# Output projection in four parts, other places for the context transposes, other banks for the last values

## The chip, the core and the metric

The kernel runs on one core of one Trainium2 chip. Its five engines have queues of their own and work in order: PE (TensorE; PEld is its weight load), DVE (VectorE), ACT (ScalarE), POOL (GpSimd) and SP (SyncE, which here only issues DMAs). They meet through semaphores. PE writes to PSUM only, and the kernel uses PSUM as five tensors: psAB, psCD and psEF of two banks each, psO and psX of one bank each. The metric is the device time in microseconds; lower is better.

## The reference, cut to what matters

Eight batches of 256 tokens with 128 features attend to a context of 512 rows with 16 heads of 64, then go through a mixture of eight experts with a capacity of 160 slots each.

```
xn  = layernorm(layernorm(x)) ; q = xn @ w_q ; k, v = split(ctx @ w_kv)      # 16 heads x 64
attn = softmax(q * 64**-0.5 @ k.T) ; out = (attn @ v) @ w_out + b_out
x   = x + tanh(g_xattn) * tanh(gate) * out
t   = layernorm(x) ; expert = argmax(softmax(t @ gate_w)) ; pos = running count inside the expert
y   = relu(t @ w1[expert]) @ w2[expert] * prob      (dropped where pos >= 160)
x   = x + tanh(g_ffn) * y
```

## The kernel before, in words

**Slots.** The two heads that share 128 columns of the weights are a pair, so a batch has 8 pairs, and the kernel has 64 slots, numbered j; hp = j % 8 is the slot's place in its batch. "Slot 1 of batch 4" is hp 1 of the batch with index 4. All engines run the same loop `batch(b)` over slots, written out by hand; the order of the calls in it is the order on the engine.

**One slot on PE.** (1) Scores of pair j for two query tiles, in psAB and psCD. (2) Small work that depends on hp, in psO: ranks in slot 0, output projection in 1 and 3, x transposes in 4, token transposes in 5, logits in 6. (3) K and Q of pair j+2 in psEF (`k_project`, `q_project`). (4) `o_transposes`: the attention output of pair j-3 is transposed into the last 256 columns of psEF. (5) `v_project`: a fourth of half the values, in psX. (6) `values`: 48 matmuls of attention times values for pair j-2, in psO. In slot 2 of a batch the transposes of the next batch's context follow in psX (`ctx_transposes`).

**One slot on DVE.** Row maximum of psAB (L913, L916), low part of the values (VL, L906) out of psX, a small drain of psO that depends on hp, row maximum of psCD, `kq_lo` (HL, L900, or a copy to KQS, L896) out of psEF, in slot 1 `add_part` and in slot 3 `add_attention` out of psO, then `normalise_heads` (L924, L930) out of psO.

**One slot on ACT.** Two exponentials out of psAB (L753), `kq_hi` (L715) out of psEF, `phi` (L763), two exponentials out of psCD, `ot_copy` (L742), `v_hi` (L720), `phi`. `kq_hi` waits for `o_transposes` of the same slot, since both use psEF. POOL makes the low half of the probabilities (L654), and SP transposes both halves by DMA (PT<-PARTS, L477), two DMAs a slot; `values` two slots later reads what they bring.

**Who may use psO.** `wait_o(free_when)` waits until the last tenant of psO has been read, and notes what will free it from the new one; `wait_x` does the same for psX. So the next tenant of psO on PE always waits for the engine that drains the last one.

**The projection.** out @ w_out sums over all 8 pairs. Before, `project_part` (L1353) takes pairs 0 to 3 of batch b-1 in slot 1 of batch b, and DVE's `add_part` (L957) adds the result to X1; `project` (L1389) takes pairs 4 to 7 in slot 3, and `add_attention` (L946) makes the new x. In the last batch the parts stand behind the slots, in psX and psEF.

Of the kernel before, what the change touches and what calls it, by code (L numbers as in the profile page):

```python
# [21 lines left out]
F32 = mybir.dt.float32  # L22
# [11 lines left out]
def gated_block(nc, x, ctx_1024, g_xattn, g_ffn, ln_gamma, ln_beta, w_q, w_kv, w_out, b_out, gate,  # L34
# [34 lines left out]
    with ExitStack() as ctx:  # L69
# [122 lines left out]

        def ps_logits(b):
            return (psX if b == B - 1 else psO)[:, 0:QT * E]

        def ps_ranks(b):
            return (psX if b == B - 1 else psO)[:, 0:(QT + 1) * E]
# [166 lines left out]
        PART_STEP, CTX_STEP, PROJECT_STEP = 1, 2, 3  # L364
        VALUES_BEHIND = 2

# [22 lines left out]

        def kq_bank(j):  # L390

            return psCD if j == 1 else psEF
# [14 lines left out]
        BO_STEP, BIAS_STEP = 2, 7  # L407
# [280 lines left out]
        def _(act):  # L688
# [15 lines left out]
            def ctxt_hi(b):  # L704
                act.wait_ge(ctxt_psum, b + 1)
                act.activation(cT_hi[:, b % 2, :], psX[:], ACT.Copy).then_inc(ctxt_hi_done, 1)
# [27 lines left out]
            def ot_copy(n, bank=psOT, pairs=1):  # L734
# [4 lines left out]
                if b:  # L739

                    act.wait_ge(part_psum if pair < PAIRS // 2 else proj_psum, b)
# [41 lines left out]
            def batch(b):  # L783
                for j, hp in slots(b):
                    if hp == CTX_STEP + 1 and not is_last(b):
# [4 lines left out]
                    if hp == CTX_STEP:  # L790
                        v_hi(*v_group(b, hp))
# [5 lines left out]
                    if hp != CTX_STEP and v_group(b, hp):  # L797
# [39 lines left out]
        def _(dve):  # L837
# [47 lines left out]
            def ctxt_lo(b):  # L885
                dve.wait_ge(ctxt_hi_done, b + 1)
                dve.tensor_tensor(cT_lo[:, b % 2, :], psX[:], cT_hi[:, b % 2, :].bitcast(F32), ALU.subtract).then_inc(ctxt_lo_done, 1)
# [30 lines left out]
            def normalise_heads(b, hp):  # L918

                j = b * PAIRS + hp  # L920
                sums = psO[:, 0:2 * QT * (DH + 1)].rearrange("p (g d) -> p g d", d=DH + 1)
                n = turn(j)
                dve.wait_ge(pv_done, n)
                dve.reciprocal(rden[:, hp % 2, :], sums[:, :, DH]).then_inc(rden_done, 1)  # L924
# [9 lines left out]
            def add_attention(b, banks=None):  # L934

                dve.wait_ge(proj_psum, b + 1)
                dve.wait_ge(part_done, B + 1 if is_last(b) else b + 1)
# [13 lines left out]
            def add_part(b, part, bank=psO):  # L951

                dve.wait_ge(part_psum, part + 1)
# [113 lines left out]
            def batch(b):  # L1067
                for j, hp in slots(b):
                    row_max(b, hp, 0)
                    if hp == CTX_STEP + 1:  # L1070
                        if not is_last(b):
                            ctxt_lo(b + 1)
                    elif j and v_group(*back(b, hp, 1)):
                        v_lo(*v_group(*back(b, hp, 1)))
                    if hp == RANKS_STEP and b > 1:
# [17 lines left out]
                    if j == LAST:  # L1093
                        low_parts()
                        place(B - 2)
# [493 lines left out]
```

## Time and profile before

| | |
|---|---|
| median of 3 runs | 491.48 us (490.69 to 491.77) |
| the profiled execution: its time, its span | 489.88 us, 487.9 us |
| busy: PE, DVE, ACT, POOL | 433.6, 367.0, 382.9, 355.7 us |
| granted TensorE clock, mean | 0.994 |

Busy time is the union of an engine's instructions, and a matmul's duration holds the filling of the pipeline, so matmuls overlap in the rows: what one costs PE is read from the starts that follow each other. In the timeline a row has start, duration, engine, line, operation, tiles and count; in brackets the idle time of the engine just before it and what ended it. "SPq" rows are the time in which SP issues a DMA, not the transfer. In the table of stretches each row begins with the stretch and its length, and the busy time of each engine follows.

### The profile page before, as it was taken

How to read it: one execution, taken by the hardware profiler on the slowest of the kernel's cores; microseconds unless marked ns; L12 is line 12 of the kernel's file. 1: busy time of each engine (PE TensorE's matmuls, PEld its weight loads, DVE VectorE, ACT ScalarE, POOL GpSimd, SP SyncE). 2: the span in 40 equal slices, each digit the busy share in tenths (PEclk: the TensorE clock that was granted, in tenths of full speed). 3: DMA queues.
4: the chain of work that ended last, by engine and by line, in shares of the span. 5: the costliest groups of instructions: out<-in, count | busy, mean ns of one | idle time of the engine just before them, and what ended most of it. 6: DMA issues, size and time to landing. Idle time of an engine off the chain costs nothing.

```text
span 487.9 us, 13156 instructions
## 1 busy us (share of the span) xinstructions
PE 433.6 (89%) x5096; PEld 334.3 (69%) x5096; DVE 367.0 (75%) x803; ACT 382.9 (78%) x616; POOL 355.7 (73%) x270
## 2 busy tenths in 40 slices
PE   8869998899889998899889989899889989888893
PEld 7647775676667776676667767677667666657893
DVE  4788886699678886789669887689669867785622
ACT  5879997699778988699788987799779986893330
POOL 3785894788867987798867987788778876681325
PEclk9998999999999999999999999999999999999999
DMA  6399999899998999999989999999989997797021
GB/s 181 128 206 174 184 205 156 162 199 196 194 184 179 193 192 170 187 186 202 190 180 176 179 186 184 195 188 196 190 129 177 192 179 138 124 165 163 14 65 44
DMA packets 283037, 82.10 MB, mean 168 GB/s; under 512 B 264387, under 2 KB 280435, under 8 KB 282976
## 3 DMA queue, kind: packets, MB, share of 16 engines
q1 hardware_dynamic: 281600, 77.96, 89.7%
q0 software_dynamic: 1376, 3.30, 2.1%
q8 instruction: 41, 0.67, 0.6%
q14 instruction: 20, 0.16, 0.1%
HBM read 10.83 MB, written 5.14 MB: 33 GB/s over the span
## 4 chain that ended last, share of the span: by engine, by line
PE 53%; DVE 18%; ACT 12%; DMA 7%; issue 6%; POOL 3%; POOLq 0%; SPq 0%; ACTq 0%; DVEq 0%
DVE MXL L913 7%; DMA PT<-PARTS 6%; PE psO L1299 5%; ACT P L753 4%; PE psAB L1267 4%; PE psO L1301 4%; ACT HL L715 4%; PE psO L1300 4%; PE psAB L1274 4%; PE psCD L1274 3%; DVE HL L900 3%; PE psEF L1193 3%; PE psO L1389 3%; PE psO L1353 3%; PE psEF L1195 2%
## 5 line engine op out<-in xcount | busy, mean ns | idle before, releaser
L654 POOL TENSOR_TENSOR PARTS<-P,PARTS 128x1024 f16<-128x1024 f32 x125 | 267.2, 2140 | 78.3 <-ACT PARTS L763 77.6
L763 ACT ACTIVATE PARTS<-P 128x1024 f16<-128x1024 f32 x126 | 135.3, 1074 | 0.8
L1299 PE MATMUL psO<-VH,PT 128*128 128x65 f16 x1008 | 99.6, 195 | 26.6 <-DVE row L946 11.5
L1299 PEld LDWEIGHTS psO<-VH,PT 128*128 128x128 f16 x1008 | 90.9, 98 | 46.6 <-DVE row L946 14.6
L753 ACT ACTIVATE P<-psAB,NB 128x512 f32<-128x512 f32 x128 | 81.5, 694 | 42.4 <-DVE NB L916 41.1
L1300 PE MATMUL psO<-VL,PT 128*128 128x64 f16 x1008 | 99.0, 193 | 0.0
L1301 PE MATMUL psO<-VH,PT 128*128 128x65 f16 x1008 | 98.8, 194 | 0.0
L913 DVE TENSOR_REDUCE MXL<-psAB 128x2 f32<-128x1024 f32 x64 | 78.3, 1223 | 19.5 <-PE psAB L1274 12.3
L1301 PEld LDWEIGHTS psO<-VH,PT 128*128 128x128 f16 x1008 | 92.0, 97 | 0.0
L1300 PEld LDWEIGHTS psO<-VL,PT 128*128 128x128 f16 x1008 | 91.9, 99 | 0.0
L753 ACT ACTIVATE P<-psCD,NB 128x512 f32<-128x512 f32 x128 | 81.0, 692 | 1.5 <-DVE NB L916 0.7
L913 DVE TENSOR_REDUCE MXL<-psCD 128x2 f32<-128x1024 f32 x64 | 77.6, 1213 | 0.2 <-PE psCD L1274 0.2
L900 DVE TENSOR_TENSOR HL<-psEF,HL 128x768 fp32r<-128x768 f32 x41 | 39.2, 955 | 26.5 <-ACT HL L715 24.7
L715 ACT ACTIVATE HL<-psEF 128x768 fp32r<-128x768 f32 x41 | 33.4, 814 | 19.0 <-PE psEF L1310 18.6
L906 DVE TENSOR_TENSOR VL<-psX,VH 128x512 f16<-128x512 f32 x63 | 42.8, 680 | 1.5 <-ACT VH L720 1.5
L1274 PE MATMUL psAB<-HL 64*128 64x512 f32 x252 | 41.2, 432 | 0.8 <-ACT P L753 0.8
L1274 PE MATMUL psCD<-HL 64*128 64x512 f32 x252 | 37.5, 402 | 4.2 <-ACT P L753 4.2
L720 ACT ACTIVATE VH<-psX 128x512 f16<-128x512 f32 x63 | 38.8, 616 | 0.0
L924 DVE RECIPROCAL rden<-psO 128x4 f32<-128x4 f32 x64 | 11.4, 179 | 35.2 <-PE psO L1301 34.6
L1193 PE MATMUL psX<-w_hi,cT_hi 128*128 128x512 f32 x63 | 30.2, 479 | 5.0 <-DVE VL L906 2.6
L742 ACT ACTIVATE OT<-psEF 128x256 f32<-128x256 f32 (+1 forms) x63 | 25.1, 399 | 9.1 <-PE psEF L1310 7.2
L1274 PEld LDWEIGHTS psCD<-HL 64*128 64x128 f32 x252 | 22.5, 186 | 14.3 <-ACT P L753 10.2
(228 smaller groups left out, 876.5 us busy)
## 6 DMA issues: line engine op xcount, KB each, us to landing
ctx_raw<-in_ctx_dram SPq DMA_DIRECT2D x8, 256.0 KB, 3.6
w1s<-in_L_ffn_w_dram SPq DMA_DIRECT2D x8, 256.0 KB, 3.4
w2s<-in_L_ffn_w_dram SPq DMA_DIRECT2D x8, 256.0 KB, 4.4
PT<-PARTS SPq DMA_TRANSPOSE x126, 4.8
experts_table<-zeros POOLq DMA_DIRECT2D x2, 645.0 KB, 4.1
X<-in_x_dram SPq DMA_DIRECT2D x8, 128.0 KB, 4.0
wraw<-in_L_xattn_w_kv_dram SPq DMA_DIRECT2D x4, 256.0 KB, 5.1
out_dram<-row SPq DMA_DIRECT2D x8, 128.0 KB, 2.8
```

Source lines behind the costliest of these rows:

```text
L654: pool.tensor_tensor(PARTS[:, par, qt, 1], P32[:, par, qt], PARTS[:, par, qt, 0], ALU.subtract).then_inc(plo_done, 1)
L715: act.activation(HL[:, hp % 2, H_KHI:H_KHI + KQ], kq_bank(j)[:, 0:KQ], ACT.Copy).then_inc(kq_hi_done, 1)
L753: last = act.activation(P32[:, par, qt, SK * h:SK * h + SK], score_bank(qt)[:, SK * h:SK * h + SK], ACT.Exp, bias=NB[:, par, qt, h:h + 1])
L763: act.activation(PARTS[:, hp % 2, qt, 0], P32[:, hp % 2, qt], ACT.Copy).then_inc(phi_done[qt], 1)
L900: dve.tensor_tensor(hl[:, H_KLO:H_KLO + KQ], kq_bank(j)[:, 0:KQ], hl[:, H_KHI:H_KHI + KQ].bitcast(F32), ALU.subtract).then_inc(kq_done, 1)
L906: dve.tensor_tensor(VL[:, kt, 8 * half:8 * half + 8, :], bank[:].rearrange("p (h d) -> p h d", d=DH), VH[:, kt, 8 * half:8 * half + 8, 0:D ...
L913: dve.tensor_reduce(MXL[:, par, qt, :, 0], score_bank(qt)[:].rearrange("p (h n) -> p h n", h=2), AX.X, ALU.max, negate=True).then_inc(max_ ...
L1193: pe.matmul(dst, hi_l, hi_r, start=True, stop=False)
L1274: last = pe.matmul(score_bank(qt)[:, SK * h:SK * h + SK], hl[rows, q + P * qt:q + P * qt + P], hl[rows, k:k + SK], start=(q == H_QHI and k ...
L1299: pe.matmul(psO[:, g:g + DH + 1], phi, VH[:, kt, head, 0:DH + 1], start=first_, stop=False)
L1300: pe.matmul(psO[:, g:g + DH], phi, VL[:, kt, head, :], start=False, stop=False)
L1301: last = pe.matmul(psO[:, g:g + DH + 1], plo, VH[:, kt, head, 0:DH + 1], start=False, stop=last_)
```

## The change

1. The projection is made in four parts of two pairs each. Parts 0 and 1 (pairs 0, 1 and 2, 3) stand in slots 5 and 7 of the batch itself, part 2 (pairs 4, 5) in slot 1 of the next batch, and the rest (pairs 6, 7, with `add_attention`) in slot 3. PE does each behind K and Q and ahead of `o_transposes`; before, it did them ahead of K and Q.
2. DVE does `add_part` and `add_attention` right behind the second row maximum, ahead of `kq_lo`; before, behind it.
3. The context transposes of batches 1 to 7 go to psO, behind the scores of slot 2, ahead of K and Q. ACT's `ctxt_hi` moves from slot 3 to the head of slot 2, DVE's `ctxt_lo` from slot 3 to slot 2. With this `v_hi` and `v_lo` of slot 2 stand where they stand in every other slot.
4. In the last batch: logits and ranks of batch 6 use psEF; the part of eight matmuls behind the last scores is gone (slots 5 and 7 hold it now); `values` of the last pair goes to psX.
5. POOL adds the projection's bias to X1 in slot 4 instead of slot 7, and `ot_copy` waits for the part that reads its place.

```diff
-        PART_STEP, CTX_STEP, PROJECT_STEP = 1, 2, 3
+        CTX_STEP, PROJECT_STEP = 2, 3
+        PART_STEPS = {5: (0, 0), 7: (0, 1), 1: (1, 2)}
+        PARTS_A_BATCH = 3
+        def part_of(b, hp):
+            late, n = PART_STEPS.get(hp, (0, None))
+            return None if n is None or b < late else (b - late, n)
+        def part_pairs(n):
+            return range(2 * n, 2 * n + 2)
+        def ctx_bank(b):
+            return psO if b else psX
-        BO_STEP, BIAS_STEP = 2, 7
+        BO_STEP, BIAS_STEP = 2, 4
...
 # ACT, batch()
-                    if hp == CTX_STEP + 1 and not is_last(b):
+                    if hp == CTX_STEP and not is_last(b):
                         ctxt_hi(b + 1)
...
 # DVE, batch()
+                    if part_of(b, hp):
+                        add_part(*part_of(b, hp))
+                    if hp == PROJECT_STEP and not is_first(b):
+                        add_attention(b - 1)
                     if not (is_last(b) and hp + AHEAD >= PAIRS):
                         kq_lo(*next_pair(b, hp, AHEAD))
-                    if hp == PART_STEP and not is_first(b):
-                        add_part(b - 1, b - 1)
-                    if hp == PROJECT_STEP and not is_first(b):
-                        add_attention(b - 1)
...
 # PE
-            def project_part(b, pairs, bank=psO):
+            def project_part(b, n, bank=psO):
+                pairs = part_pairs(n)
                 if bank is psO:
-                    wait_o((part_done, b + 1))
+                    wait_o((part_done, PARTS_A_BATCH * b + n + 1))
                 pe.wait_ge(ot_done, b * PAIRS + pairs[-1] + 1)
                 pe.wait_ge(wo_in, 16)
...
 # PE, batch()
-                    if hp == PART_STEP and not is_first(b):
-                        project_part(b - 1, range(PAIRS // 2))
-                    if hp == PROJECT_STEP and not is_first(b):
-                        project(b - 1)
+                    if hp == CTX_STEP and not is_last(b):
+                        ctx_transposes(b + 1)
...
                         q_project(*next_pair(b, hp, AHEAD))
+                    if part_of(b, hp):
+                        project_part(*part_of(b, hp))
+                    if hp == PROJECT_STEP and not is_first(b):
+                        project(b - 1)
...
 # PE, behind the last slot
                     values(b, PAIRS - 3)
-                    project_part(b, range(PAIRS // 2), psX)
-                    values(b, PAIRS - 1)
+                    values(b, PAIRS - 1, psX)
```

PE in slot 1 of batch 4, before: the projection (psO<-wo,OT) stands between the scores (psCD<-HL) and K and Q (psEF).

```order
L1274 MATMUL psCD<-HL 128x512 x6
L1353 MATMUL psO<-wo,OT 128x128 x8
L1193 MATMUL psEF<-cT_hi,w_hi 128x512
L1194 MATMUL psEF<-cT_lo,w_hi 128x512
L1195 MATMUL psEF<-cT_hi,w_lo 128x512
L1193 MATMUL psEF<-xT_hi,w_hi 128x256
L1194 MATMUL psEF<-xT_lo,w_hi 128x256
L1195 MATMUL psEF<-xT_hi,w_lo 128x256
L1310 MATMUL psEF<-ident,O 128x128 x2
```

The same place now:

```order
L1292 MATMUL psCD<-HL 128x512 x6
L1211 MATMUL psEF<-cT_hi,w_hi 128x512
L1212 MATMUL psEF<-cT_lo,w_hi 128x512
L1213 MATMUL psEF<-cT_hi,w_lo 128x512
L1211 MATMUL psEF<-xT_hi,w_hi 128x256
L1212 MATMUL psEF<-xT_lo,w_hi 128x256
L1213 MATMUL psEF<-xT_hi,w_lo 128x256
L1373 MATMUL psO<-wo,OT 128x128 x4
L1328 MATMUL psEF<-ident,O 128x128 x2
```

The projection has moved behind the six matmuls of K and Q and has four matmuls instead of eight.

DVE in slot 1 of batch 4, before: from the row maximum of psCD to the normalisation (rden, O); HL is `kq_lo`, X<-psO is `add_part`.

```order
L913 TENSOR_REDUCE MXL<-psCD 128x2
L916 TENSOR_REDUCE NB<-MXL 128x2
L900 TENSOR_TENSOR HL<-psEF,HL 128x768
L957 SCALAR_TENSOR_TENSOR X<-psO,gscale,X 128x256
L924 RECIPROCAL rden<-psO 128x4
L930 TENSOR_TENSOR O<-psO,rden 128x2x2x64
```

The same place now:

```order
L931 TENSOR_REDUCE MXL<-psCD 128x2
L934 TENSOR_REDUCE NB<-MXL 128x2
L978 SCALAR_TENSOR_TENSOR X<-psO,gscale,X 128x256
L918 TENSOR_TENSOR HL<-psEF,HL 128x768
L944 RECIPROCAL rden<-psO 128x4
L950 TENSOR_TENSOR O<-psO,rden 128x2x2x64
```

`add_part` and `kq_lo` have changed places; slot 3 differs in the same way for `add_attention`, and slots 5 and 7 gain an `add_part` at this place.

ACT in slot 2 and the beginning of slot 3 of batch 4, before: cT_hi is `ctxt_hi`, VH is `v_hi`.

```order
L753 ACTIVATE P<-psAB,NB 128x512 x2
L715 ACTIVATE HL<-psEF 128x768
L720 ACTIVATE VH<-psX 128x8x64
L763 ACTIVATE PARTS<-P 128x1024
L753 ACTIVATE P<-psCD,NB 128x512 x2
L742 ACTIVATE OT<-psEF 128x256
L763 ACTIVATE PARTS<-P 128x1024
L706 ACTIVATE cT_hi<-psX 128x512
L753 ACTIVATE P<-psAB,NB 128x512 x2
```

The same slot now:

```order
L723 ACTIVATE cT_hi<-psO 128x512
L773 ACTIVATE P<-psAB,NB 128x512 x2
L732 ACTIVATE HL<-psEF 128x768
L783 ACTIVATE PARTS<-P 128x1024
L773 ACTIVATE P<-psCD,NB 128x512 x2
L762 ACTIVATE OT<-psEF 128x256
L737 ACTIVATE VH<-psX 128x8x64
L783 ACTIVATE PARTS<-P 128x1024
```

`ctxt_hi` has moved from the end of the slot to its head, ahead of the first exponentials, and `v_hi` from ahead of the second exponentials to behind them.

## Rows read from the trace of the kernel before

**Rows 1.** Stretches of batch 4: slots 1 and 3, and all eight slots.
```profile
232.38:241.35 8.97, 7.33 (x87) 5.79 (x85) 5.22 (x9) 7.22 (x11) 6.87 (x6) 1.00 1.16 187
...
248.06:257.43 9.37, 7.72 (x93) 6.14 (x89) 5.99 (x16) 6.88 (x11) 6.89 (x6) 1.00 0.73 153
...
sum 53.90, PE 49.42 PEld 37.33 DVE 43.06 ACT 46.08 POOL 43.43; mean PE 6.18 PEld 4.67 DVE 5.38 ACT 5.76 POOL 5.43
```

**Rows 2.** Timeline of PE in slot 1 of batch 4: start, duration, what.
```profile
232.96 2.05 PE L1353 MATMUL psO<-wo,OT 128*128 128x128 f32 x16
234.77 0.47 PE L1193 MATMUL psEF<-cT_hi,w_hi 128*128 128x512 f32 x1
...
236.59 0.40 PE L1195 MATMUL psX<-w_hi,cT_lo 128*128 128x512 f32 x1
...
238.63 0.20 PE L1299 MATMUL psO<-VH,PT 128*128 128x65 f16 x1 [1.65 <-DVE X L957]
...
240.17 0.70 PE L1267 MATMUL psAB<-wraw 64*128 64x512 f32 x2
```

**Rows 3.** Timeline of DVE and ACT in slot 1 of batch 4.
```profile
235.56 0.16 DVE L916 TENSOR_REDUCE NB<-MXL 128x2 f32<-128x4 f32 x1
237.22 0.96 DVE L900 TENSOR_TENSOR HL<-psEF,HL 128x768 fp32r<-128x768 f32 x1 [1.51 <-ACT HL L715]
238.10 0.47 DVE L957 SCALAR_TENSOR_TENSOR X<-psO,gscale,X 128x256 f32<-128x256 f32 x1
...
236.38 0.81 ACT L715 ACTIVATE HL<-psEF 128x768 fp32r<-128x768 f32 x1 [1.29 <-PE psEF L1310]
```

**Rows 4.** Waits: who waited, for whom, total us, times, longest.
```profile
PE psO L1299 <- DVE row L946: 11.5, 7, 1.7
PE psO L1299 <- DVE X L957: 11.5, 7, 1.7
...
PE psX L1219 <- DVE VL L906: 3.9, 6, 0.7
...
PEld psO L1299 <- DVE winners L994: 1.4, 1, 1.4
```

**Rows 5.** Timeline of PE in slot 3 of batch 7: second scores.
```profile
409.58 0.96 PE L1274 MATMUL psCD<-HL 64*128 64x512 f32 x6 [0.65 <-ACT P L753]
```

**Rows 6.** Timeline of DVE in slot 5 of batch 4.
```profile
264.79 0.41 DVE L883 COPY tT<-psO 128x256 f32<-128x256 f32 x1
...
266.36 0.16 DVE L916 TENSOR_REDUCE NB<-MXL 128x2 f32<-128x4 f32 x1
```

**Rows 7.** Timeline of SP's queue, slots 1 to 7 of batch 4 and beyond.
```profile
245.42 1.55 SPq L452 DMA_DIRECT2D X<-in_x_dram  x1
...
253.08 0.80 SPq L484 DMA_DIRECT2D ctx_raw<-in_ctx_dram  x1
...
260.77 1.85 SPq L459 DMA_DIRECT2D w2s<-in_L_ffn_w_dram  x2
...
268.88 1.00 SPq L448 DMA_DIRECT2D out_dram<-row  x1
...
281.57 0.73 SPq L459 DMA_DIRECT2D w2s<-in_L_ffn_w_dram  x1
282.40 17.42 SPq L477 DMA_TRANSPOSE PT<-PARTS  x6
```

**Rows 8.** Batch 0: SP's issue of w_out, its landing on the page, PE in slot 5.
```profile
47.54 0.61 SPq L489 DMA_DIRECT2D wo<-in_L_xattn_w_out_dram  x1
...
wo<-in_L_xattn_w_out_dram SPq DMA_DIRECT2D x1, 512.0 KB, 5.3
...
49.61 0.38 PE L1310 MATMUL psEF<-ident,O 128*128 128x128 f32 x2
```

**Rows 9.** Timeline behind the last slot: DVE's last low half, PE's last values.
```profile
442.90 1.21 DVE L1020 TENSOR_TENSOR wraw<-psCD,wraw 128x1024 f16<-128x1024 f32 x1
...
447.16 0.20 PE L1299 MATMUL psO<-VH,PT 128*128 128x65 f16 x1 [0.48 <-DVE O L930]
```

More of the change, by code:

```diff
@@ L948, in add_attention, with add_part @@
                                          op1=ALU.add).then_inc(x1_done, 1)
-            def add_part(b, part, bank=psO):
+            def add_part(b, n, bank=psO):
+                part = PARTS_A_BATCH * b + n
                 dve.wait_ge(part_psum, part + 1)
@@ L1069, in batch @@
                     row_max(b, hp, 0)
[L1070 to L1073, printed above, removed]
+                    if j and v_group(*back(b, hp, 1)):
                         v_lo(*v_group(*back(b, hp, 1)))
+                    if hp == CTX_STEP and not is_last(b):
+                        ctxt_lo(b + 1)
                     if hp == RANKS_STEP and b > 1:
@@ L1276, in scores, with values @@
                 last.then_inc(score_psum, 1)
-            def values(b, hp):
+            def values(b, hp, bank=psO):
                 j = b * PAIRS + hp
                 par = hp % 2
-                wait_o((norm_done, turn(j)))
+                (wait_x if bank is psX else wait_o)((norm_done, turn(j)))
                 if j == 0:
@@ L1298, in values @@
                             first_, last_ = kt == 0, kt == KT - 1
-                            pe.matmul(psO[:, g:g + DH + 1], phi, VH[:, kt, head, 0:DH + 1], start=first_, stop=False)
-                            pe.matmul(psO[:, g:g + DH], phi, VL[:, kt, head, :], start=False, stop=False)
-                            last = pe.matmul(psO[:, g:g + DH + 1], plo, VH[:, kt, head, 0:DH + 1], start=False,
+                            pe.matmul(bank[:, g:g + DH + 1], phi, VH[:, kt, head, 0:DH + 1], start=first_, stop=False)
+                            pe.matmul(bank[:, g:g + DH], phi, VL[:, kt, head, :], start=False, stop=False)
+                            last = pe.matmul(bank[:, g:g + DH + 1], plo, VH[:, kt, head, 0:DH + 1], start=False,
                                              stop=last_)
@@ L1387, in project @@
                     dst = psO[:, D * qt:D * qt + D]
-                    for pair in range(PAIRS // 2, PAIRS):
-                        last = pe.matmul(dst, OT[:, pair * QT + qt, :], wo[:, pair, :], start=(pair == PAIRS // 2),
+                    for pair in range(PAIRS - 2, PAIRS):
+                        last = pe.matmul(dst, OT[:, pair * QT + qt, :], wo[:, pair, :], start=(pair == PAIRS - 2),
                                          stop=(pair == PAIRS - 1))
```

59 lines of the change are left out of this document (33 added, 26 removed).

## The prediction

> **What bounds the kernel now.** I read the table of stretches first, slot by slot over one batch in the steady part. The reader is to see there that the slots are not alike: slot 1 takes 8.97 us and slot 3 9.37 us, the other six (53.90 - 8.97 - 9.37) / 6 = 5.93 us on the mean, and that PE, the busiest engine, is busy for 49.42 of the batch's 53.90 us [rows 1]. So PE sets the pace, with 4.48 us of gaps a batch, and the long slots are where the gaps should be looked for. The timeline of PE in slot 1 then shows where. The projection takes PE from 232.96 to the start of K at 234.77, 1.81 us for 16 instructions (8 matmuls, each in two passes); the last V matmul starts at 236.59, and the values start only at 238.63, after 1.65 us without work, released by DVE's `add_part`. The values then hold PE until 240.17, 1.54 us [rows 2]. Third, DVE and ACT at the same place tell why the add is late: DVE is done with the second row maximum at 235.56 + 0.16 = 235.72, but the instruction next in its queue is `kq_lo`, and that waits 1.51 us for ACT's `kq_hi`, which itself waited 1.29 us for the transposes behind K and Q. The add, 0.47 us long, stands behind it and starts at 238.10 [rows 3]. Its own operand, the projection, was ready before K began at 234.77. The list of waits shows that this is not one slot: 11.5 us over 7 slots behind `add_part`, 11.5 us over 7 behind `add_attention`, and 3.9 us over 6 for the context transposes, which wait until DVE has emptied psX [rows 4].
>
> **The change part by part, ordinary batches (1 to 6).** PE's work stays the same: 16 projection matmuls a batch before (8 and 8), 16 now (4 in each of four slots), so the 0.91 us (half of 1.81) that slots 1 and 3 each lose, slots 5 and 7 each gain. What changes is waits.
>
> *Slot 1.* With four matmuls fewer the last V matmul starts at 236.59 - 0.91 = 235.68 and is through some 0.23 later (the step from one 512-column matmul to the next), at 235.9. DVE is free for the add at 235.72, its operand is there (the part now stands ahead of the transposes and V, which are nearly through by then), and it ends at 235.72 + 0.47, with the handing over about 236.25. So the values begin at about 236.2 to 236.3 instead of 238.63, and of the 1.65 us wait about 0.3 is left; in a slot whose V is a little later less. I take 0.2 for each of the four slots with a part. What is late next is DVE's add itself, not `kq_lo`: that now ends behind the start of the values, beside 1.54 us of them. Queued behind the add on DVE are `kq_lo` (wanted by the scores two slots on) and the normalisation, which waits for the values anyway; both have that cover, and without it the 0.47 us would show once a slot.
>
> *Slot 3.* The same edit, the same wait: 1.65 us goes, 0.2 stays.
>
> *Slots 5 and 7.* Their 0.91 us of matmuls are already in the balance of PE's work. In slot 5 the part may only enter psO when DVE has copied the token transposes, at 264.79 + 0.41 = 265.20. Behind it PE has 0.91 us of part and about 0.9 of transposes and V (an estimate: K, Q, transposes and V take 236.59 + 0.23 - 234.77 = 2.05 together [rows 2]), so it wants the values' bank at about 267.0. DVE's second row maximum ends at 266.36 + 0.16 = 266.52 [rows 6], the add at about 267.05: the copy and the add cost PE no more than they do in slot 1. Slot 7 has no other tenant in psO. The bounds for the wait in each of the four slots are nothing and the present 1.65; near 0.2 is where the rows of slots 1 and 5 both put it.
>
> *Slot 2.* The context transposes wanted psX empty and waited 0.65 us (3.9 over 6) [rows 4]; in psO they stand behind the scores, and the normalisation before them is done meanwhile, so that wait goes. ACT pays: `ctxt_hi` must now wait until PE has done scores and transposes, ahead of the first exponentials, while `v_hi` no longer stands ahead of the second ones. If these come late, the second scores of slot 3 wait for them. In batch 7, where slot 2 has no context transposes and is short already, such a wait is seen, 0.65 us [rows 5]. Its bounds are nothing and that 0.65; I take 0.35, near the middle.
>
> *SP and DMA.* Nothing is added to SP's queue, but it must keep up. Bounds: nothing from below, 1.3 a batch from above (rival 1); I take 0.3, nearer to the low end, since the change makes the fast slots 5 and 7 slower and so evens out the demand.
>
> Sum of an ordinary batch: -1.65 - 1.65 - 0.65 + 4 x 0.2 + 0.35 + 0.3 = -2.5 us, over six batches -15.0.
>
> **Batch 0.** Here the change adds a wait that no other batch has. Part 0 now needs w_out in slot 5 of batch 0; SP issues that load at 47.54 and such a load lands 5.3 us later, about 52.85, while PE reaches the place of the part at 49.61 [rows 8]. That is 3.2 us of stall, with everything of PE queued behind it: the transposes for `kq_lo`, V, and the values of the slot. The parts of slots 5 and 7 add 0.91 us each, and slots 1 and 3 of this batch have none to lose. SP's queue is solid in that stretch and catches up meanwhile, so I give back 0.6: 3.2 + 1.8 - 0.6 = +4.4. The bounds are +1.5 (the stall wholly given back by later slots that wait for transposes now) and +5.0.
>
> **Batch 7 and the tail.** Slots 1 and 3: two waits less the 0.4 that stay, -2.9, and half of each projection gone, -1.8. Slot 5 +0.95. Slot 6: the logits leave psO, and the values no longer wait for DVE's reading of them (1.4 us on PE's weight load [rows 4], of which I take 0.8, since transposed probabilities land hardly earlier). Slot 7's part stands where PE waits for the last exponentials: nothing. Behind the slots, the eight-matmul part goes, and the values of the last pair enter psX instead of waiting for psO. They then wait for the last low half, at 442.90 + 1.21 = 444.11, for their second half alone, and end at about 444.11 + 0.1 + 0.77 = 445.0; with 0.38 for a pair of transposes (as in rows 8) the next values start at 445.4 instead of 447.16 [rows 9], -1.8. Sum -2.9 - 1.8 + 0.95 - 0.8 - 1.8 = -6.35.
>
> Moving the bias on POOL from slot 7 to slot 4 costs nothing: it stands there ahead of an idle wait for `phi`, and the first reader is slot 5; without that cover it would be one 128x256 addition a batch.
>
> Total: -15.0 + 4.4 - 6.35 = -16.95. Against the profiled execution's own time of 489.88 us (487.9 of span and 2.0 around it) that is 472.9; the median of the runs, 491.48, lies 1.6 above, so 474.5.
>
> **Rivals.**
> 1. *SP's queue becomes the bound.* From 282.40 to 299.82 SP issues six transposes one behind the other, 17.42 us, 2.90 each. Sixteen a batch take 46.5 us, and the other issues (1.55 + 0.80 + 1.85 + 1.00 + 0.73 = 5.9) make it 52.4 [rows 7]. PE's own need by my sum is 53.90 - 2.8 = 51.1 before any wait for DMA. If SP can't do better when pressed, a batch gains 1.5, not 2.5: -9.0, with batch 0 at +3.3 (the parts hide in it) and batch 7 at -5.4: -11.1, 480. Against it: the stretch is the fullest of the batch, and slots of even length press the queue less.
> The Trainium skill bears on this in "Perfetto Trace Analysis", section "What 'DMA-bound' means": a kernel is DMA-bound on the sequencer when the issuing engine's track is solid DMA slices. The trace has such a track in the stretch named, not in slots 1 to 4. The skill's "DMA: Bandwidth & Descriptors", section "Latency and other measured facts", gives 261 GB/s for a DMA transpose; the 512 KB of one would take 2.0 us by it, an estimate from that page, and a batch 38 us, which binds nothing and leaves 474.5. The 2.90 us measured here decide, so the rival stays.
> 2. *All gaps of PE close.* 53.90 - 49.42 = 4.48 a batch, -26.9 in six, batch 7 -8.0 (its 6.35 and the waits left in it), batch 0 +3.3: -31.6, 460. For it speaks that the gaps named are nearly all there are; against it, ACT (46.08 us busy a batch [rows 1]) and SP have little room for it.
> 3. *psO becomes a serial bank, and it is slower.* psO has four projections, the context and the small work now, each to be drained before the values. If in each slot w us of wait stay, a batch changes by -3.95 + 4w: from w = 1.0 on it gains nothing, and with w = 1.65, the present wait, it loses 2.65. Over seven batches +18.6, with the stall of batch 0 and the tail +20: 512. What would do it is DVE reaching the second row maximum late in these slots. Against it: in slots 1 and 5 DVE is done with it before PE's V would be through.
> The Trainium skill speaks for this rival ("Perfetto Trace Analysis", section "Matmuls"): independent matmul groups should rotate through different banks, so that the drain of one overlaps the next. By that rule the parts belong in another bank; the trace shows K, Q and V, which use psEF and psX, between part and values, and that is the cover the price w depends on.
> 4. *No change*: batch 0's stall and SP's queue eat the gain, 491.
>
> **How the numbers follow.** The forecast, 468 to 480, has 0.55; SP's queue (480, up to 486) 0.20; all gaps closed (460) 0.15; psO serial (512) 0.07; no change 0.03. Faster by over 0.2% (about what a measurement of this kernel can tell from no change): 0.55 + 0.20 + 0.15 = 0.90; same 0.03; slower 0.07. The range 463 to 485 leaves out the last two, half of the closed gaps and the edge of SP's case, just under 0.2.
>
> **What would show it.** In the profile after, slots 1 and 3 should be about 6.5 us long, slots 5 and 7 about 6.6; the waits of the values for `add_part` and `add_attention` should be under 0.5 us each; PE should stand still for about 3 us near 50 us, waiting for w_out; SP's queue should be fuller. I am wrong if the values wait over 1 us for the add in slots 5 or 7, if the values wait for transposes all along, or if slot 2 is longer than 6.7 us.

## The result and the profile after

The changed kernel takes 471.93 us (median of 4 runs, 470.05 to 474.06) where the kernel before, run beside it, takes 491.41. The ratio is 0.9607, 95% interval 0.9561 to 0.9652. The profiled execution took 471.12 us, of which 469.1 are span. A few runs of some kernels were slow (over 1.5% above the fastest of the same kernel, at a lower granted clock): the medians below are of all runs, the ratios leave the slow ones out, and the profile of experiment 3 is of one of them.

First the table of stretches of batch 4, slots 1, 3, 5, 6 and 7 and the sum of all eight, which answers to [rows 1].

```profile
229.20:235.73 6.53, 6.21 (x77) 4.69 (x75) 5.23 (x11) 6.34 (x12) 4.54 (x5) 1.00 0.98 191
...
241.49:248.77 7.28, 6.98 (x85) 5.46 (x85) 6.08 (x16) 6.66 (x13) 6.56 (x5) 1.00 1.13 187
...
254.19:261.06 6.87, 6.72 (x83) 5.59 (x85) 5.50 (x10) 6.84 (x13) 6.87 (x6) 1.00 1.02 226
261.06:268.55 7.49, 6.16 (x75) 4.52 (x73) 5.34 (x14) 5.31 (x9) 5.74 (x3) 1.00 1.19 184
268.55:275.31 6.76, 6.76 (x78) 4.61 (x75) 5.87 (x14) 5.36 (x11) 4.38 (x4) 1.00 1.36 201
sum 51.78, PE 49.54 PEld 37.16 DVE 44.00 ACT 44.94 POOL 42.79; mean PE 6.19 PEld 4.64 DVE 5.50 ACT 5.62 POOL 5.35
```

PE's work is unchanged (49.54 us against 49.42), and the batch is 2.1 us shorter. Slots 1 and 3 have lost 2.4 and 2.1 us, slots 5 and 7 are longer. Slot 6 is new among the long ones: 7.49 us, with PE busy for only 6.16.

PE in slot 1 of batch 4, which answers to [rows 2]: the part, the last V matmul, the first of the values.

```profile
230.72 1.05 PE L1373 MATMUL psO<-wo,OT 128*128 128x128 f32 x8
...
232.29 0.40 PE L1213 MATMUL psX<-w_hi,cT_lo 128*128 128x512 f32 x1
233.01 0.20 PE L1317 MATMUL psO<-VH,PT 128*128 128x65 f16 x1 [0.32 <-DVE X L978]
```

DVE at the same place, which answers to [rows 3].

```profile
232.36 0.16 DVE L934 TENSOR_REDUCE NB<-MXL 128x2 f32<-128x4 f32 x1
232.47 0.48 DVE L978 SCALAR_TENSOR_TENSOR X<-psO,gscale,X 128x256 f32<-128x256 f32 x1
232.93 0.96 DVE L918 TENSOR_TENSOR HL<-psEF,HL 128x768 fp32r<-128x768 f32 x1
```

The add now follows the second row maximum at once, and PE stands for 0.32 us where it stood for 1.65. `kq_lo` begins when the values do.

The list of waits (engine, tile and line, for whom: us in total, times, longest) answers to [rows 4]. A wait of the values is booked on PE or, where the weight load was held, on PEld.

```profile
PEld psCD L1292 <- ACT P L773: 15.2, 24, 2.0
...
PEld psO L1317 <- DVE X L978: 9.6, 21, 0.8
...
PE psO L1317 <- DMA PT<-PARTS: 5.2, 9, 1.1
PE psCD L1292 <- ACT P L773: 5.1, 15, 1.6
...
PE psO L1373 <- DMA wo<-in_L_xattn_w_out_dram: 4.3, 1, 4.3
...
PEld psO L1317 <- DVE row L966: 1.9, 7, 0.3
...
PE psO L1317 <- DVE X L978: 1.6, 5, 0.3
```

Before, the weight load's line beside the 11.5 us of PE was:

```profile
PEld psO L1299 <- DVE X L957: 14.6, 7, 2.1
```

The waits for the adds are short. One wait can stand in both lists: before, a wait of 1.65 us on PE was 2.08 on the weight load, so 0.4 us on the weight load costs PE nothing. Of the 21 waits for `add_part` on the weight load, five are waits of PE too, 0.33 us each, in slot 1 of batches 2 to 6. PE's timeline says the same: from V's last matmul to the first of the values it takes 0.24 us in a slot without an add, and in these batches 0.72 in slot 1, 0.36 in slot 7 and 0.24 in slots 3 and 5.

One wait is new, and one has grown. PE waits 4.3 us, once, for w_out. And the values wait for transposed probabilities 9 times, 5.2 us in all, up to 1.1; in the trace of before this line reads 1.7 us, 4 times. Slot 6 of batch 4 holds two of them, in PE's timeline:

```profile
264.90 0.19 PE L1317 MATMUL psO<-VH,PT 128*128 128x65 f16 x1 [0.58 <-DMA PT<-PARTS]
...
266.54 0.20 PE L1317 MATMUL psO<-VH,PT 128*128 128x65 f16 x1 [0.76 <-DMA PT<-PARTS]
```

The wait for w_out has a second price. These two stretches, from 47.2 and from 52.1 us, show it (behind the length stand the busy times of PE, PEld, DVE, ACT and POOL, then the granted clock):

```profile
47.20:51.50 4.30, 0.02 (x1) 0.00 (x0) 1.14 (x2) 3.13 (x5) 4.30 (x3) 1.00 0.98 196
52.10:55.40 3.30, 3.30 (x25) 2.68 (x24) 1.44 (x2) 0.69 (x2) 0.00 (x0) 0.50 1.19 145
```

PE stands still in the first, and in the second the granted clock is 0.50, the 1.2 of the two levels 1.2 and 2.4 GHz: V's matmuls start 0.43 us apart there, against 0.23 in slot 1 of batch 4.

SP's queue in and behind batch 4, which answers to [rows 7], has few gaps:

```profile
224.04 18.91 SPq L494 DMA_TRANSPOSE PT<-PARTS  x6
...
256.52 1.14 SPq L476 DMA_DIRECT2D w2s<-in_L_ffn_w_dram  x2
257.76 6.86 SPq L494 DMA_TRANSPOSE PT<-PARTS  x2
...
276.86 17.41 SPq L494 DMA_TRANSPOSE PT<-PARTS  x6
```

A row of six holds the gaps between its issues too: the six from 224.04 are 15.9 us of issue in 18.9, those from 276.86 are 16.0 in 17.4, so 2.6 to 2.7 each. I add up SP's issues from batch to batch, without gaps: in batches 2 to 5 they fill 92 to 95% of the time, in the kernel before 79 to 85%. The mean issue of a transpose grows from 2.45 to 2.73 us in these batches. And the queue is behind what feeds it: over batches 1 to 6, POOL's low half is done 0.73 us before SP begins its transpose (the median; 0.02 in the kernel before), so it is not POOL that is late.

Measured from one row maximum of psAB to the next, the slots have lengths that repeat to 0.1 us where nothing disturbs them. Means over batches 1 to 6, and the usual length of after:

| slot | 0 | 1 | 2 | 3 | 4 | 5 | 6 | 7 | batch |
|---|---|---|---|---|---|---|---|---|---|
| before | 5.69 | 8.96 | 6.71 | 9.37 | 5.43 | 5.84 | 6.01 | 5.80 | 53.80 |
| after | 5.63 | 6.53 | 5.78 | 7.35 | 5.62 | 6.87 | 6.26 | 7.08 | 51.12 |
| after, undisturbed | 5.67 | 6.53 | 5.77 | 7.25 | 5.43 | 6.87 | 5.82 | 6.76 | 50.10 |

So the span's 18.8 us come from batches 1 to 6 (-16.1), batch 7 and what follows (-7.4), batch 0 (+4.3) and the start (+0.4).

### The profile page after: what moved, and what is told of

Read it like the earlier page. It is cut to its first block, busy times and chain, and to the rows that moved or that the text cites. A ratio compares the mean times of both kernels' runs of the same rounds, so it can differ in the third digit from the quotient of the medians.

```text
span 469.1 us, 13202 instructions
## 1 busy us (share of the span) xinstructions
PE 434.6 (93%) x5096; PEld 334.6 (71%) x5096; DVE 372.3 (79%) x818; ACT 383.3 (82%) x616; POOL 355.1 (76%) x270
## 4 chain that ended last, share of the span: by engine, by line
PE 36%; DVE 18%; POOL 17%; DMA 10%; issue 9%; ACT 9%; SPq 1%; POOLq 0%; ACTq 0%; DVEq 0%
POOL PARTS L671 14%; DMA PT<-PARTS 8%; DVE MXL L931 7%; ACT P L773 4%; PE psO L1317 3%; PE psAB L1285 3%; PE psO L1373 3%; PE psO L1319 2%; PE psO L1318 2%; DVE HL L918 2%; PE psCD L1285 2%; PE psCD L1292 2%; PE psEF L1211 2%; PE psEF L1549 2%; DVE VL L924 2%
## 5 line engine op out<-in xcount | busy, mean ns | idle before, releaser
L773 ACT ACTIVATE P<-psAB,NB 128x512 f32<-128x512 f32 x128 | 81.7, 698 | 25.1 <-DVE NB L934 24.9
L1292 PE MATMUL psCD<-HL 64*128 64x512 f32 x252 | 38.5, 410 | 5.3 <-ACT P L773 5.1
L944 DVE RECIPROCAL rden<-psO 128x4 f32<-128x4 f32 x63 | 11.4, 180 | 27.5 <-PE psO L1319 27.1
```

The lines of the kernel that those rows point to most:

```text
L773: last = act.activation(P32[:, par, qt, SK * h:SK * h + SK], score_bank(qt)[:, SK * h:SK * h + SK], ACT.Exp, bias=NB[:, par, qt, h:h + 1])
L1292: last = pe.matmul(score_bank(qt)[:, SK * h:SK * h + SK], hl[rows, q + P * qt:q + P * qt + P], hl[rows, k:k + SK], start=(q == H_QHI and k ...
```

## The experiments

All times are medians; the ratios are to the kernel before on the same chip, with their 95% intervals. "After" is 0.9607. What is read from a profile is read from one execution of each kernel.

**1. The order on DVE alone, in the kernel before.**

```diff
 # DVE, batch()
+                    if hp == PART_STEP and not is_first(b):
+                        add_part(b - 1, b - 1)
+                    if hp == PROJECT_STEP and not is_first(b):
+                        add_attention(b - 1)
                     if not (is_last(b) and hp + AHEAD >= PAIRS):
                         kq_lo(*next_pair(b, hp, AHEAD))
                     if hp == CTX_STEP:
                         v_lo(*v_group(b, hp))
-                    if hp == PART_STEP and not is_first(b):
-                        add_part(b - 1, b - 1)
-                    if hp == PROJECT_STEP and not is_first(b):
-                        add_attention(b - 1)
```

> The kernel before with one edit: DVE does add_part and add_attention ahead of kq_lo; the projection stays in two parts of eight matmuls, ahead of K and Q, in slots 1 and 3. Theory (the late add in DVE's queue is the cause of the long slots): both 1.65 us waits of the values vanish, in seven batches 23 us at the most; some of it comes back as waits for transposed probabilities, since SP's queue has less slack: 468 to 476 us, with no wait for w_out in batch 0. Rival (the split into four, or the place behind K and Q, is what helps): the values then wait for something else in slots 1 and 3, and the time stays above 484 us.

473.56 us, 0.9636 (0.9598 to 0.9673). In the list of waits the two lines of 11.5 us are gone, and this line has come up:

```profile
PE psO L1299 <- DMA PT<-PARTS: 8.5, 12, 1.7
```

Four moved lines give nearly all that the whole change gives; the intervals of the two overlap. Undisturbed, slots 1 and 3 are 7.16 and 7.56 us long, 1.8 less each than before, and the sum of the eight is 50.1, as in the kernel after. With eight matmuls on PE the add is done before V is through: the values follow V's last matmul by 0.24 us in slots 1 and 3, as in a slot without an add, so no wait is left.

**2. The old order on DVE, in the kernel after.**

```diff
-                    if part_of(b, hp):
-                        add_part(*part_of(b, hp))
...
-                    if hp == PROJECT_STEP and not is_first(b):
-                        add_attention(b - 1)
                     if not (is_last(b) and hp + AHEAD >= PAIRS):
                         kq_lo(*next_pair(b, hp, AHEAD))
+                    if part_of(b, hp):
+                        add_part(*part_of(b, hp))
+                    if hp == PROJECT_STEP and not is_first(b):
+                        add_attention(b - 1)
```

> The kernel after with one edit: the adds are put back behind kq_lo on DVE, all four of a batch. Theory (the place in DVE's queue is the price of a tenant of psO): each of the 28 adds makes the values wait about 1.4 us longer, 39 us in all, some of it beside waits that are there anyway: 500 to 512 us, slower than the kernel before. Rival (the parts of four matmuls are early enough for the old order too): under 10 us on 472.

507.23 us, 1.0350 (1.0327 to 1.0372), slower than the kernel before. PE's first values and DVE's add in slot 1 of batch 4:

```profile
251.61 0.20 PE L1317 MATMUL psO<-VH,PT 128*128 128x65 f16 x1 [1.65 <-DVE X L978]
```

```profile
250.20 0.96 DVE L918 TENSOR_TENSOR HL<-psEF,HL 128x768 fp32r<-128x768 f32 x1 [0.41 <-ACT HL L732]
251.08 0.47 DVE L978 SCALAR_TENSOR_TENSOR X<-psO,gscale,X 128x256 f32<-128x256 f32 x1
```

The same 1.65 us as in the kernel before, with half the matmuls, and in slots 1, 3 and 7 instead of two (0.8 in slot 5): batches of 55.9 us. The wait belongs to the place in DVE's queue, and the split alone makes it worse.

**3. w_out loaded at the start.**

```diff
             sp.dma_start(ctx_raw[:], ctx_t[1]).then_inc(ctx_in, 16)
+            sp.dma_start(wo[:], w_out.rearrange("(c p) n -> p c n", p=P)).then_inc(wo_in, 16)
...
-                    if is_first(b) and hp == WO_STEP:
-                        sp.dma_start(wo[:], w_out.rearrange("(c p) n -> p c n", p=P)).then_inc(wo_in, 16)
```

> The kernel after with one edit: SP issues the load of w_out at the start, behind the second context, and not in slot 5 of batch 0. Theory (the stall of PE for w_out in batch 0 is lost time): it goes, 4.3 us in the trace, so 3.3 to 4.3 us faster than the kernel after, about 468 us. Rival (PE's stall lets SP's queue catch up, and SP sets the pace behind it): the waits for transposes take its place, and the gain is under 1.5 us.

465.29 us, 0.9499 (0.9462 to 0.9535). Slot 5 of batch 0 falls from 12.52 to 6.38 us, and the time by about 5 (0.0108 of 490). The stall was lost time, and SP's catching up did not pay for it. It cost 6.1 us of slot 5 where PE stood for 4.3; in this profile the granted clock stays 1.00 there, and the other 1.8 us are about what 3.4 us at half the clock lose, so I put them down to the clock of 0.50 behind the stall.

**4. The context transposes at their old place, in psX at the end of slot 2** (with `ctxt_hi`, `ctxt_lo`, `v_hi` and `v_lo` as before).

```diff
-            return psO if b else psX
+            return psX
...
-                    if hp == CTX_STEP and not is_last(b):
-                        ctx_transposes(b + 1)
                     if hp == X_STEP and not is_last(b):
...
                         values(*back(b, hp, VALUES_BEHIND))
+                    if hp == CTX_STEP and not is_last(b):
+                        ctx_transposes(b + 1)
```

> The kernel after with one edit: the context transposes go back to the end of slot 2 in psX, with ctxt_hi and ctxt_lo in slot 3 and v_hi, v_lo of slot 2 at their old places. Theory (the wait for psX was lost time): 0.65 us in each of six or seven batches comes back, and the ACT wait in slot 3 (0.3) goes: +2 to +4 us, 474 to 476. Rival (SP's queue now sets the pace, and what PE gains in slot 2 is lost in waits for transposes): within 1 us of the kernel after.

474.21 us, 0.9664 (0.9630 to 0.9697): 2.8 us above after by the ratios, but the intervals overlap, so the time does not show it. The wait for psX is back:

```profile
PE psX L1242 <- DVE VL L926: 4.4, 7, 0.7
```

Slot 2 grows from 5.77 to 6.72 us and slot 3 shrinks from 7.25 to 6.94, 0.6 us a batch in all. The 0.3 us in slot 3 is the price that ACT pays. That is without disturbance. As they ran, batches 1 to 6 are 51.26 us on the mean, against 51.12 in after, and the values wait 2.2 us for transposes here, 5.2 in after: most of what the place in psO saves was lost there again, as the rival said. And 4.7 of the 5.7 us by which this profile's span is longer lie in batch 0, where the granted clock fell to 0.50 twice more than in after.

**5. The last values in psO again.**

```diff
-            normalise_heads(B - 1, PAIRS - 1, psX)
+            normalise_heads(B - 1, PAIRS - 1)
...
-                    values(b, PAIRS - 1, psX)
+                    values(b, PAIRS - 1)
```

> The kernel after with one edit: the values of the very last pair go to psO again, as in the kernel before. Theory (they then wait until the normalisation has emptied psO): the stretch from the last row maximum of psAB to the end, 50.50 us in the profile after and 52.00 in that of before, grows by 1.0 to 1.8 us, and the time with it: 473 to 474. Rival (the last values wait for the last low half in any case): 0 to 0.4 us.

472.57 us, 0.9629 (0.9594 to 0.9665): the time can't tell it from after. The profile can: the stretch from the last row maximum of psAB to the end is 52.42 us, against 50.50.

**6. The parts ahead of K and Q** (slots 1, 3 and 7; with the early w_out of experiment 3).

```diff
+                    if hp != TOKT_STEP and part_of(b, hp):
+                        project_part(*part_of(b, hp))
+                    if hp == PROJECT_STEP and not is_first(b):
+                        project(b - 1)
...
                         k_project(*next_pair(b, hp, AHEAD))
                         q_project(*next_pair(b, hp, AHEAD))
-                    if part_of(b, hp):
+                    if hp == TOKT_STEP and part_of(b, hp):
                         project_part(*part_of(b, hp))
-                    if hp == PROJECT_STEP and not is_first(b):
-                        project(b - 1)
```

> The kernel with the early load of w_out (465.3 us) with one more edit: PE does the parts of slots 1 and 7 and the rest of slot 3 ahead of K and Q, as before; slot 5 stays behind. Theory (the 0.3 us that the values wait for each add come from the place behind K and Q): three waits of 0.3 go in each batch, slots 1, 3 and 7 become 6.2, 6.9 and 6.5 us, up to 6 us in all, of which waits for transposes may take half: 460 to 463. Rival (SP's queue sets the pace): as much more waiting for transposes, under 1.5 us of gain.

465.25 us, 0.9482 (0.9448 to 0.9515): nothing gained on experiment 3. I was wrong on why: the slots keep their lengths, and the wait its 0.32 us, in slot 1 of batch 3. On PE, then on DVE:

```profile
172.51 1.16 PE L1372 MATMUL psO<-wo,OT 128*128 128x128 f32 x8
...
175.95 0.20 PE L1316 MATMUL psO<-VH,PT 128*128 128x65 f16 x1 [0.32 <-DVE X L977]
```

```profile
175.30 0.16 DVE L933 TENSOR_REDUCE NB<-MXL 128x2 f32<-128x4 f32 x1
175.41 0.48 DVE L977 SCALAR_TENSOR_TENSOR X<-psO,gscale,X 128x256 f32<-128x256 f32 x1
```

The part is done at 173.67, the add still comes late: DVE has the second row maximum to end first, so the place of the part on PE doesn't matter. There was less to gain than I expected, too: a wait of PE for the add stands in slot 1 and, by 0.1 us, in slot 7, and none in slot 3.

**7. Two parts of eight matmuls again** (batches 0 to 6, slots 1 and 3, ahead of K and Q; all else as after; parts in slots 5 and 7 in the last batch only).

```diff
-        PART_STEPS = {5: (0, 0), 7: (0, 1), 1: (1, 2)}
-        PARTS_A_BATCH = 3
+        LAST_PARTS = {5: 0, 7: 1}
...
+            if hp == 1 and not is_first(b):
+                return (b - 1, 0)
+            return (b, LAST_PARTS[hp]) if is_last(b) and hp in LAST_PARTS else None
...
+            return range(2 * n, 2 * n + 2) if is_last(b) else range(PAIRS // 2)
...
```

> The kernel after with the projection of batches 0 to 6 in two parts of eight matmuls again (slots 1 and 3, ahead of K and Q), with the new order on DVE, the new place of the context and the new tail; only the last batch has parts in slots 5 and 7. Theory (the split into four gives an ordinary batch nothing and costs a wait for each add more; w_out isn't wanted in batch 0): an ordinary batch is 50.1 - 0.95 + 0.34 = 49.5 us without disturbance, batch 0 some 49; 462 to 466 us, as fast as the kernel with the early load of w_out. Rival (four short parts spread PE's work and spare SP's queue): 468 us or more.

476.14 us, 0.9708 (0.9662 to 0.9754). My theory fell. Undisturbed, a batch is 49.8 us long (5.67, 7.16, 5.88, 8.16, 5.43, 5.83, 5.88, 5.80), 0.3 shorter than after, but the mean is 51.7, for:

```profile
PE psO L1318 <- DMA PT<-PARTS: 13.4, 13, 2.6
```

That is 1.9 us a batch of disturbance against 1.0 in after, nearly all of it in slots 6 and 7. Slots 4 to 7 of this kernel take 22.9 us undisturbed, and in batches 2 to 5 SP's issues in them add up to 23.9 to 27.5 us, so the queue can't keep up there. In the kernel after the same slots take 24.9 us, with 24.9 to 26.6 us of issues. So the four short parts cost 0.3 us a batch, and the kernel with them is faster; that they save by evening out the demand fits these sums but was not tested by itself. Part of the disturbance is PE's clock. In batch 2 PE waits for transposes until 168.9 us, and behind that the granted clock is 0.50 for 3.4 us:

```profile
166.60:168.90 2.30, 0.05 (x2) 0.00 (x0) 0.70 (x1) 2.30 (x5) 1.56 (x1) 1.00 1.32 82
169.10:172.40 3.30, 3.30 (x30) 2.18 (x28) 1.22 (x6) 1.01 (x2) 2.48 (x2) 0.50 1.15 244
```

Slot 7 of this batch takes 9.55 us instead of 5.80.

**8. SP's queue.** Five kernels on its load. First, experiment 3 with the eight loads of w2 issued in the very last slot (`if j == LAST`) instead of slots 3 and 6 of batches 3 to 6:

```diff
-                        for piece in range(first, min(first + PIECES[hp], 2 * E)):
+                        for piece in range(first, min(first + PIECES[hp], E)):
                             expert_piece(piece)
+                    if j == LAST:
+                        for piece in range(E, 2 * E):
+                            expert_piece(piece)
```

> The kernel with the early load of w_out (465.3 us) with one more edit: SP issues the eight loads of w2 in the last slot, behind all transposes, and not in slots 3 and 6 of batches 3 to 6. Theory (SP's queue, and what it moves, is what the values wait for in slots 6 and 7): batches 3 to 6 come down to the sum of their undisturbed slots, 50.1 us from 51.1 on the mean; 2 to 4 us faster, and the runs lie closer together. Rival (the transposes alone fill the queue, or the disturbance is none of SP's): under 1 us.

467.65 us, 0.9550 (0.9511 to 0.9589), so not faster. Batches 3 to 6, which had held the loads of w2, came down to 50.5 us on the mean, from 51.2 in after (batches 1 and 2, with the loads of w1 as before: 50.7, from 50.9), but the stretch behind the last row maximum grew from 50.5 to 55.4: the first gathering of rows now stood behind the loads in SP's queue.

```profile
PE psAB L1519 <- DMA PARTS<-experts_table: 3.1, 1, 3.1
```

Of the 4.9 us more this wait is 3.1, and from 427.3 to 434.2 us, in and behind this wait, the granted clock was 0.50.

Then experiment 6 with 21 loads more, and the kernel before with the same 21:

```diff
...
                             expert_piece(piece)
+                        for n in range(PIECES[hp]):
+                            if extra[n]:
+                                sp.wait_ge(extra_in[n], 16 * extra[n])
+                            extra[n] += 1
+                            sp.dma_start(scratch[:, n, :], w1[0]).then_inc(extra_in[n], 16)
```

> The kernel with the early w_out and the parts ahead of K and Q (465.3 us) with 21 added loads of 256 KB that nothing reads: as many as there are loads of weights, in slots 3 and 6 of batches 1 to 7. Theory (SP's queue is full in that kernel): each takes 0.7 us or more of a queue that was 83 to 97% busy; batches 2 to 5 grow by 2 us each, the others by 1: 473 to 479 us. Rival (the queue has room, PE and DVE set the pace): 465 to 467.

> The kernel before with the same 21 added loads that nothing reads. Theory (in the kernel before, SP's queue was 71 to 85% busy in batches 1 to 6 and the long slots hid it): 0 to 3 us on 490. Rival (SP's queue costs in the kernel before as much as in the faster one): 8 to 14 us more.

480.16 us, 0.9774 (0.9740 to 0.9808), on the fast kernel: 14 to 15 us more (0.9774 - 0.9482 = 0.029 of 490). 493.30 us, 1.0042 (1.0013 to 1.0070), on the kernel before: 2 us. The first values of slot 6 in batch 4 of the fast kernel:

```profile
268.69 0.19 PE L1325 MATMUL psO<-VH,PT 128*128 128x65 f16 x1 [2.24 <-DMA PT<-PARTS]
```

The same loads cost 0.7 us each in the one and 0.1 in the other. A full queue is not by itself a cost: in the kernel before, the added loads bring SP's issues to 89 to 94% of batches 2 to 6, and a transpose is ready 0.86 us before SP begins it (the median, as above), longer than in after; but this kernel's slots are longer, and the values wait for transposes 4.4 us in all. In the fast kernel they wait 16.6 us, a transpose is ready 1.38 us before SP begins it, and the granted clock fell to 0.50 twice behind such waits, for 10.2 us in all.

Last, experiment 6 with the weights' loads thinned out (one of w1 a batch) and w2 behind the first gathering of rows, PE waiting for w2 only ahead of `down(0)`:

```diff
-                    if b and hp in PIECES:
-                        first = 3 * (b - 1) + (2 if hp == LOGITS_STEP else 0)
-                        for piece in range(first, min(first + PIECES[hp], 2 * E)):
-                            expert_piece(piece)
+                    if b and hp == 3:
+                        expert_piece(b - 1)
+                    if b == 1 and hp == 6:
+                        expert_piece(E - 1)
...
+            for piece in range(E, 2 * E):
+                expert_piece(piece)
             x1_store(B - 1)
...
             def down(e):
+                if e == 0:
+                    pe.wait_ge(w2_in, 16 * E)
...
-            pe.wait_ge(w2_in, 16 * E)
```

> The kernel with the early w_out and the parts ahead of K and Q (465.3 us) with the expert weights moved out of the way of the transposes: one load of w1 a batch in slot 3 of batches 1 to 7 (and one in slot 6 of batch 1) in place of three in each of batches 1 to 3, and the eight loads of w2 behind the first gathering of the experts' rows, with PE waiting for w2 only at the first expert's second product. Theory (SP's queue is the limit that is left): batches 1 to 6 come to 50.1 to 50.5 us each and the tail stays 50.5: 461 to 463.5 us. Rival (the loads cost nothing where they were): 465, or more if the late loads hold up the tail.

462.09 us, 0.9415 (0.9396 to 0.9434): the fastest of all, 2% below after. A batch takes 50.45 us on the mean, from 50.94 in experiment 6, and the waits for transposes are down from 4.1 us to

```profile
PE psO L1318 <- DMA PT<-PARTS: 3.1, 5, 1.2
```

The same edit in the two-part kernel of experiment 7:

> The kernel with two parts of eight matmuls in batches 0 to 6 (476.1 us) with the expert weights moved as in the kernel of 462.1 us. Theory (that kernel has shorter undisturbed slots, 49.3 us a batch against 50.1, and loses to the four parts only by waits for transposes in slots 6 and 7, which fewer loads in SP's queue shorten): 465 to 470 us. Rival (with the queue relieved, the shorter slots decide, and two parts beat four): under 462. Second rival (the loads have nothing to do with its waits): 474 or more.

468.51 us, 0.9567 (0.9527 to 0.9606) (the 49.3 us of the expectation took the shortest slots seen; the usual ones make 49.8): 7 us gained, as the theory said, and still 6 to 7 behind the four parts, with 13 waits for transposes, 10.7 us in all. So the loads are one part of what the values wait for, and most of it is there without them. None of these kernels tells SP's issuing from the transfers behind it, since each load moved or added is both; the transposes were not tried from another engine's queue.

## Why the prediction was right

It forecast 474.5 us; 471.93 came. The mechanism in slots 1 and 3 held, and most terms of the sum lie near theirs. Two do not, SP's and batch 0's, and that the total fits in spite of them is partly luck.

*Slots 1 and 3.* The step held: the add behind `kq_lo` was the whole wait. By its terms slot 1 becomes 8.97 - 1.65 - 0.91 + 0.2 = 6.6 us and slot 3 9.37 - 2.56 + 0.2 + 0.35 = 7.4; they are 6.53 and 7.25 undisturbed. The sign that I gave, "slots 1 and 3 about 6.5", was wrong for slot 3 by the prediction's own arithmetic, as was "about 6.6" for slots 5 and 7. The waits under 0.5 us came true: over the four slots 0.48, 0, 0 and 0.12 us beyond the usual 0.24, 0.15 on the mean where 0.2 was taken. Experiment 1 shows what the prediction did not see: the order on DVE alone is enough, and the 0.3 us wait of PE in slot 1 is made by the split, since four matmuls fewer leave the add without cover.

*What is late next is DVE's add, not `kq_lo`.* Right, and experiment 6 shows that not even an earlier part helps.

*Slots 5 and 7.* +0.91 + 0.2 each, so 6.95 and 6.91; measured 6.87 and 6.76. DVE's rows in slot 5 stand where [rows 6] put them: row maximum done, add directly behind.

```profile
257.70 0.16 DVE L934 TENSOR_REDUCE NB<-MXL 128x2 f32<-128x4 f32 x1
257.81 0.48 DVE L978 SCALAR_TENSOR_TENSOR X<-psO,gscale,X 128x256 f32<-128x256 f32 x1
```

*Slot 2 and the start of slot 3.* -0.65 and +0.35 were taken, -0.95 and +0.31 came (experiment 4, undone) in undisturbed slots; whether the time gains by it, experiment 4 leaves open. The second scores of slot 3 wait for ACT as [rows 5] had shown them to in batch 7:

```profile
241.77 0.96 PE L1292 MATMUL psCD<-HL 64*128 64x512 f32 x6 [0.32 <-ACT P L773]
```

*SP and DMA.* This is the mis-sized term: 0.3 us a batch, measured about 1.0 (51.12 against 50.10 undisturbed; 0.1 in the kernel before). That the slots' gains were larger by 0.8 made up for it, so an ordinary batch gained 2.68 us where 2.5 was forecast. The upper bound of 1.3 rested on a misread row. The 17.42 us from 282.40 in [rows 7] hold 1.07 us in which SP waits for POOL, so a transpose took 2.73 us and not 2.90; sixteen of them and the 5.9 us of other issues make 49.6, under PE's 51.1 and not 52.4. Experiment 8 shows that the loads on SP's queue cost time in the fast kernel; whether by their issue or by their transfers is not shown. That longer slots 5 and 7 even out the demand fits experiment 7 and the last of experiment 8, where two parts lose, but is argued.

*Batch 0.* +4.4 forecast, +4.3 measured, by luck. Slot 5 grew by 6.8 us (5.68 to 12.52), where the stall of 3.2 and the part of 0.9 were taken, and slots 2 and 3 shrank by 3.1, which no term held. The shrinking is not the change's alone: in the profile of before PE stood for 2.4 us between these slots, waiting for DVE's `ctxt_lo`, with the granted clock at 0.50 from 38.4 to 41.8 us behind it, and the two took 17.3 us; in experiment 1, with the context at the same place, they took 14.7 without that wait. The stall of PE was 4.32 us rather than 3.2: SP issued the load 1.1 us sooner than in [rows 8], but PE was at the place of the part 2.4 us sooner, at 51.54 - 4.32 = 47.22 where the prediction took 49.61. And the clock of 0.50 behind the stall, which the prediction did not price, brought the loss to 6.1 (experiment 3).

```profile
46.39 0.58 SPq L506 DMA_DIRECT2D wo<-in_L_xattn_w_out_dram  x1
```

```profile
51.54 1.56 PE L1373 MATMUL psO<-wo,OT 128*128 128x128 f32 x8 [4.32 <-DMA wo<-in_L_xattn_w_out_dram]
```

PE could begin 5.15 us after the issue, against the 5.3 taken.

*Batch 7 and the tail.* -6.35 forecast, -7.4 measured: slot 1 -2.4, slot 3 -3.15 (its ACT wait of [rows 5] fell from 0.65 to 0.18), slot 5 +1.05, slot 6 -0.5 where 0.8 was taken, the stretch behind the slots -1.5 where 1.8 was taken, and slot 0 -0.8, which was disturbed in the profile of before and in no term. Behind the slots, as forecast, the next values start 1.04 us after DVE's last low half ends; in [rows 9] it was 3.05.

```profile
426.13 1.22 DVE L1041 TENSOR_TENSOR wraw<-psCD,wraw 128x1024 f16<-128x1024 f32 x1
```

```profile
428.39 0.19 PE L1317 MATMUL psO<-VH,PT 128*128 128x65 f16 x1
```

*The rivals.* Rival 1 came in part, on top of the forecast rather than in its place: SP's queue or the transfers behind it are the limit that is left, but at 50.5 to 51.8 us a batch, not at 52.4, since pressed transposes took 2.7 to 2.8 us on the mean and not 2.9 throughout. Rival 2 is what the undisturbed slots show: 3.7 of the 4.5 us of gaps did close, and SP gave one back. Rival 3 was priced well: experiment 2 realises it, with 507 us where 512 was worked out from w = 1.65; the batch of 55.9 us gives w = (55.9 - 53.9 + 3.95) / 4 = 1.5. It was averted by the order on DVE, which the prediction had read from [rows 3]. The rule of the Trainium skill ("Perfetto Trace Analysis", section "Matmuls") that independent groups should rotate through banks has its price here as a range: 0 to 0.5 us a tenant where the drain stands ahead of `kq_lo` on DVE, 1.0 to 1.8 where it stands behind it (experiment 2).

What stays open: why two even parts lose more to the transposes than the four, in detail. Experiment 7 and the last of experiment 8 show that they do and where they wait; that the run of four short slots is the reason is argued from their lengths.

## What to carry to other kernels

Where a wait names a short drain, look at what stands ahead of it in its engine's queue: moving four lines was worth 18 us here, and the split and the banks around it a few more at most, which show in the time only with w_out loaded earlier. When PE's gaps close, ask at once what the queue that feeds PE does in that stretch; a load that cost 0.1 us before cost 0.7 afterwards. Look at the first iteration by itself, since an operand loaded late can cost there what is gained in two others; and price a long wait of PE with the clock behind it: the 4.3 us for w_out cost 6.1.

## What was not expected

The issue of a transpose on SP is no constant. Its mean over a batch (1 to 6) was 2.2 to 2.6 us in the kernel before, 2.5 to 2.8 in the kernel after and up to 3.0 with the added loads, so that SP's queue fills faster than the work on it grows.

A long wait of PE can be followed by a lower clock. In the profiles of experiments 3, 7 and 8 (the added loads) waits for transposes of 2.1 to 2.5 us have a granted clock of 0.50 for 3.4 to 6.8 us behind them, and the wait comes first. Not every wait has: the one of 2.6 us up to 320.3 in experiment 7 has none. The runs of one kernel scatter (469.5 to 479.9 us in experiment 1, 463.5 to 465.8 in experiment 6, 488.4 to 493.7 in the kernel before, run beside it), and so do their granted clocks; how much of the one is the other was not settled.
